# Self-attention of a perceiver: two batches at a time in tiles of 64 rows and columns, instead of one batch with two heads stacked

## The reference

```python
def _L0_attn_ref(x, qkv_w, proj_w, proj_b, slopes):      # head size 16
    q, k, v = (x @ qkv_w.T) split and by head             # rotary on q and k
    attn = einsum('bhqd,bhkd->bhqk', q, k) * 16 ** -0.5
    attn = attn + minimum(key - query, 0) * slopes[h] * 8.0
    out = einsum('bhqk,bhkd->bhqd', softmax(attn), v)
    return out @ proj_w.T + proj_b

def _L1_attn_ref(x, Wq, Wk, Wv, Wo):                      # head size 64
    scores = einsum('bhqd,bhkd->bhqk', Q, K) / 8          # rotary on Q and K
    scores = where(|query - key| <= 16, scores, -inf)
    return einsum('bhqk,bhkd->bhqd', softmax(scores), V) @ Wo
```

## Time and profile before

| what | value |
|---|---|
| time, median of 3 runs | 5175.37 us (5174.06 to 5181.66) |
| the profiled execution: its own time | 5172.16 us |
| its span | 5170.4 us |
| mean granted clock of PE | 0.928 |
| `attend_batches`, tag a0: PE's first product to the end of ACT's last copy | 829.4 to 943.6 us |
| `attend_batches`, tag a1: the same | 2702.9 to 2881.3 us |

### The profile page before, as it was taken

How to read it: one execution, slowest core, us unless ns; L and a number is a source line. 1 busy time by engine, 2 the same in 40 slices (tenths; PEclk the granted TensorE clock), 3 DMA queues, 4 the chain that set the end, 5 groups by cost and what they waited for, 6 DMA issues and landing times. The chain is left out here.

```text
span 5170.4 us, 144361 instructions
## 1 busy us (share of the span) xinstructions
PE 4547.7 (88%) x65130; PEld 3576.7 (69%) x65130; DVE 2497.3 (48%) x4406; ACT 1971.9 (38%) x3916; POOL 605.4 (12%) x392
## 2 busy tenths in 40 slices
PE   6999988699999799999799579999962669999968
PEld 5777776588888577888646447777742558888744
DVE  3555545566666455555434425555525145555531
ACT  3554541233333344444303114555431134444430
POOL 1111101000000011111031011111102021111000
PEclk9999996699999899999898799999975889999979
DMA  1111100121111111111000011111012511111000
GB/s 65 41 41 39 37 15 14 38 66 49 49 49 47 57 35 42 37 41 42 34 19 0 17 36 40 41 41 41 28 24 75 201 62 35 42 42 36 23 19 18
DMA packets 86893, 216.58 MB, mean 42 GB/s; under 512 B 28240, under 2 KB 51536, under 8 KB 83584
## 3 DMA queue, kind: packets, MB, share of 16 engines
q1 hardware_dynamic: 85536, 205.51, 12.3%
q0 software_dynamic: 768, 2.10, 0.1%
HBM read 198.26 MB, written 9.32 MB: 40 GB/s over the span
## 5 line engine op out<-in xcount | busy, mean ns | idle before, releaser
L679 DVE TENSOR_REDUCE x_pm<-banks 128x4 f32<-128x1536 f32 (+2 forms) x512 | 935.6, 1827 | 687.9 <-PE banks L582 687.9
L776 ACT ACTIVATE x_pl<-banks 128x384 f32<-128x384 f32 x1536 | 628.8, 498 | 705.3 <-PE banks L565 705.3
L506 POOL TENSOR_TENSOR x_cl<-xnT,x_ch 128x1601 fp32r<-128x1601 f32 x120 | 400.6, 3339 | 3291.2 <-ACT x_ch L791 3291.2
L781 ACT ACTIVATE x_kT<-banks,x_bk 128x384 f32<-128x384 f32 (+2 forms) x512 | 305.1, 596 | 560.6 <-PE banks L593 560.6
L603 PE MATMUL banks<-x_wh,x_ch 128*128 128x256 f32 (+1 forms) x1664 | 490.6, 295 | 0.0
L593 PE MATMUL banks<-x_ch,x_wh 128*128 128x384 f32 (+2 forms) x1024 | 410.7, 401 | 87.7 <-POOL x_v L513 86.6
L565 PE MATMUL banks<-x_q,x_kT 32*128 32x128 f32 x13312 | 482.3, 277 | 3.6 <-issue 3.6
L582 PE MATMUL banks<-x_kT,x_q 32*128 32x384 f32 (+2 forms) x4096 | 457.6, 511 | 13.8 <-DVE x_v L711 9.0
L603 PE MATMUL banks<-x_wh,x_cl 128*128 128x256 f32 (+1 forms) x1664 | 469.2, 282 | 0.0
L603 PE MATMUL banks<-x_wl,x_ch 128*128 128x256 f32 (+1 forms) x1664 | 467.7, 281 | 0.0
L565 PEld LDWEIGHTS banks<-x_q,x_kT 32*128 32x128 f32 x13312 | 436.2, 185 | 7.8 <-issue 5.2
(11 more groups left out here) (341 smaller groups left out, 7207.1 us busy)
## 6 DMA issues: line engine op xcount, KB each, us to landing
xnT<-in_ctxT SPq DMA_DIRECT2D x120, 800.5 KB, 4.3
e_w<-in_L_pack SPq DMA_DIRECT2D x91, 384.0 KB, 3.1
e_w<-in_L_pack SPq DMA_DIRECT2D x21, 1154.0 KB, 5.6
actT<-in_ctxT SPq DMA_DIRECT2D x8, 800.5 KB, 7.4
e_rw<-routed_rows SPq DMA_DIRECT2D x64, 64.0 KB, 2.8
x_rows<-e_zero SPq DMA_DIRECT2D x1, 2688.0 KB, 9.8
e_xt<-x_rows SPq DMA_DIRECT2D x21, 128.0 KB, 5.3
y_rows<-e_y SPq DMA_DIRECT2D x21, 128.0 KB, 1.7
```

The costliest lines, as they stand in the source:

```text
L506: nc.gpsimd.tensor_tensor(cl[:, u, k, 0:CTX], staged(b, k), ch[:, u, k, 0:CTX], ALU.subtract).then_inc(low_done, 1)
L679: nc.vector.tensor_reduce(pm[:, c, :, g], src[:, :, 0:hi - lo], AX.X, ALU.max).then_inc(max_done, 1)
L776: nc.scalar.activation(probabilities(c, j, lo, hi).rearrange("p t q -> p (t q)"), mine[j][:, 0:(hi - lo) * P], ACT.Exp).then_inc(exp_done, 1)
L781: nc.scalar.activation(kT[:, c, lo:hi], mine[1 if g == 0 and inside(b if c else b - 1) else 0][:, 0:hi - lo], ACT.Identity, bias=col[:, c: ...
```

## The change

`attend_batches` is replaced by `attend_pairs`, and the host's arrangement of four weight arrays changes with it.

- A step takes two batches. The 128 partitions of the scores are the 64 queries of one batch and the 64 of the other, and the free axis has all 16 heads: 128 x 1024.
- The scores are 32 products per pair of batches (L929), each one head of one batch: in a1 64 rows by 64 columns with 64 moving columns, in a0 32 rows by 64 columns. The scale goes into the DVE instruction that adds the bias (L995 in a0, L999 in a1). In a0 the masked copies of the queries are made once for all batches (`qm`, L1047); in a1 there are none, and the bias is read from `dist` by all heads. There is nothing left for POOL.
- The values of all 16 batches are made ahead of the first scores (L935), each batch in two halves of the heads, which lie on partitions 0 to 63 and 64 to 127; ACT copies them to `v` (L1050).
- The probabilities of a pair are transposed in 8 blocks (L945) and copied out of PSUM by ACT (L1056), not DVE. The product by the values is 32 products of 64 rows by 64 columns (L957), with 16 moving columns in a0 and 64 in a1.
- DVE scales the result in one instruction (L1019), and PE transposes it back (`turn_back`, L966: 2 blocks in a0, 8 in a1) in place of the product by `stack2`; ACT writes it out (L1042).
- The loop over the batches is written out. The value weights lie in `net.qT`, and come in two DMAs.

The core of the diff (the removed function is the one printed above):

```diff
-        attend_batches(net, tag, width, chunks, wts[4], extra_bias, qT, kT, ahead)
+        attend_pairs(net, tag, width, chunks, wts[4], extra_bias, qT, kT, ahead)
...
+    BLOCKS = HEADS // 2
+    F = BLOCKS * width
+    N = B // 2
...
+        x_ps = net.ps[2]
+        o_ps = net.ps[3].rearrange("p (o n) -> p o n", o=2)[:, :, 0:F]
...
+            qm = net.sb(tag + "_qm", [P, 2, chunks, TOK], ctx=mem)
+            s_ps = net.quads[0][:, :, 0:4 * S].rearrange("p j (h s) -> p j h s", s=S)
+        else:
+            s_ps = net.ps[0].rearrange("p (j h s) -> p j h s", j=2, s=S)
+
+        def place(h):
+
+            if extra_bias == "alibi":
+                return h % 8 // 2, h // 8 * 2 + h % 2
+            return h % 2, h // 2
...
+        @block.tensor
+        def _(pe):
+            def scores(n):
+                if n:
+                    pe.wait_ge(biased, n)
+                elif extra_bias == "alibi":
+                    pe.wait_ge(masked, 2)
+                for h in range(HEADS):
+                    j, at = place(h)
+                    for e in range(2):
+                        tok = slice((2 * n + e) * S, (2 * n + e + 1) * S)
+                        if extra_bias == "alibi":
+                            r = slice(32 * j, 32 * j + 32)
+                            left, right = qm[r, h % 2, h // 8, tok], kT[r, h // 8, tok]
+                        else:
+                            r = slice(64 * j, 64 * j + 64)
+                            left, right = qT[r, at, tok], kT[r, at, tok]
+                        last = nc.tensor.matmul(s_ps[e * S:(e + 1) * S, j, at], left, right, start=True, stop=True)
+                last.then_inc(s_full, 1)
+
+            def values(b):
+                for half in range(2):
+                    for k in range(KC):
+                        last = nc.tensor.matmul(net.bank(b % 8)[half * S:(half + 1) * S, 0:F], net.xnT[:, k, b * S:(b + 1) * S],
+                                                w[:, half, k], start=(k == 0), stop=(k == KC - 1))
+                last.then_inc(v_full, 1)
+
+            def turn(n):
+                pe.wait_ge(p_ready, n + 1)
+                if n >= 2:
+                    pe.wait_ge(done, n - 1)
+                flat = sc[:, n % 2].rearrange("p h s -> p (h s)")
+                for i in range(BLOCKS):
+                    last = nc.tensor.transpose(x_ps[:, i * P:(i + 1) * P], flat[:, i * P:(i + 1) * P], net.ident[:])
+                last.then_inc(turned, 1)
+
+            def attend(n):
+                pe.wait_ge(pt_ready, n + 1)
+                pe.wait_ge(v_ready, 2 * n + 2)
+                if n:
+                    pe.wait_ge(o_ready, n)
+                for i in range(BLOCKS):
+                    for e in range(2):
+                        for half in range(2):
+                            r = slice(half * S, (half + 1) * S)
+                            last = nc.tensor.matmul(o_ps[e * S:(e + 1) * S, half, i * width:(i + 1) * width],
+                                                    pT[r, i, e * S:(e + 1) * S], v[r, 2 * n + e, i * width:(i + 1) * width],
+                                                    start=True, stop=True)
+                last.then_inc(o_full, 1)
+
+            def turn_back(n):
+                pe.wait_ge(o_ready, n + 1)
+                flat = o[:].rearrange("p o i f -> p (o i f)")
+                for c in range(chunks):
+                    last = nc.tensor.transpose(x_ps[:, c * P:(c + 1) * P], flat[:, c * P:(c + 1) * P], net.ident[:])
+                last.then_inc(back_turned, 1)
+
+            pe.wait_ge(w_in, 32)
+            for b in range(B):
+                if b >= 8:
+                    pe.wait_ge(v_ready, b - 7)
+                values(b)
+            pe.wait_ge(v_ready, B)
+            scores(0)
+            for n in range(N):
+                turn(n)
+                if n + 1 < N:
+                    scores(n + 1)
+                if n:
+                    pe.wait_ge(pt_ready, n + 1)
+                    turn_back(n - 1)
+                attend(n)
+            pe.wait_ge(done, N - 1)
+            turn_back(N - 1)
+
+        @block.vector
+        def _(dve):
+            def shift_scores(n):
+                u = n % 2
+                dve.wait_ge(s_full, n + 1)
+                if n >= 2:
+                    dve.wait_ge(turned, n - 1)
+                if extra_bias == "alibi":
+                    nc.vector.scalar_tensor_tensor(sc[:, u].rearrange("p (j h) s -> p j (h s)", j=4), net.quads[0][:, :, 0:4 * S],
+                                                   0.25, bias[:].rearrange("p (j h) s -> p j (h s)", j=4), ALU.mult,
+                                                   ALU.add).then_inc(biased, 1)
+                else:
+                    nc.vector.scalar_tensor_tensor(sc[:, u], net.ps[0].rearrange("p (h s) -> p h s", s=S), 0.125,
+                                                   spread(dist[:].unsqueeze(1), (P, HEADS, S)), ALU.mult,
+                                                   ALU.add).then_inc(biased, 1)
+                dve.wait_ge(biased, n + 1)
+                nc.vector.tensor_reduce(mx[:], sc[:, u], AX.X, ALU.max).then_inc(maxed, 1)
+                dve.wait_ge(maxed, n + 1)
+                nc.vector.tensor_tensor(sc[:, u], sc[:, u], per_head(mx[:]), ALU.subtract).then_inc(soft, 1)
+
+            def add_up(n):
+                dve.wait_ge(p_ready, n + 1)
+                nc.vector.tensor_reduce(sums[:], sc[:, n % 2], AX.X, ALU.add).then_inc(added, 1)
+                dve.wait_ge(added, n + 1)
+                nc.vector.reciprocal(rs[:, n % 2], sums[:]).then_inc(inverted, 1)
+
+            def divide(n):
+                dve.wait_ge(o_full, n + 1)
+                dve.wait_ge(inverted, n + 1)
+                if n:
+                    dve.wait_ge(back_turned, n)
+                scale = rs[:, n % 2].rearrange("p (i o) -> p o i", o=2).unsqueeze(3)
+                nc.vector.tensor_tensor(o[:], o_ps.rearrange("p o (i f) -> p o i f", f=width),
+                                        spread(scale, (P, 2, BLOCKS, width)), ALU.mult).then_inc(o_ready, 1)
+
+            dve.wait_ge(tab_in, 32 if extra_bias == "alibi" else 16)
+            if extra_bias == "alibi":
+                nc.vector.tensor_tensor(bias[:], spread(dist[:].unsqueeze(1), (P, HEADS, S)), per_head(slopes[:]),
+                                        ALU.mult).then_inc(bias_ready, 1)
+                dve.wait_ge(bias_ready, 1)
+            shift_scores(0)
+            for n in range(N):
+                if n + 1 < N:
+                    shift_scores(n + 1)
+                add_up(n)
+                divide(n)
+
+        @block.scalar
+        def _(act):
+            def exps(n):
+                act.wait_ge(soft, n + 1)
+                nc.scalar.activation(sc[:, n % 2], sc[:, n % 2], ACT.Exp).then_inc(p_ready, 1)
+
+            def output(n):
+                act.wait_ge(back_turned, n + 1)
+                nc.scalar.activation(net.actT[:, 0:chunks, n * P:(n + 1) * P],
+                                     x_ps[:, 0:chunks * P].rearrange("p (c s) -> p c s", s=P), ACT.Copy).then_inc(done, 1)
+
+            if extra_bias == "alibi":
+                for e in range(2):
+                    nc.scalar.activation(qm[:, e], qT[:], ACT.Copy, scale=net.parity[:, 12 + e:13 + e]).then_inc(masked, 1)
+            for b in range(B):
+                act.wait_ge(v_full, b + 1)
+                nc.scalar.activation(v[:, b], net.bank(b % 8)[:, 0:F], ACT.Copy).then_inc(v_ready, 1)
+            exps(0)
+            for n in range(N):
+                act.wait_ge(turned, n + 1)
+                if n:
+                    act.wait_ge(o_full, n)
+                nc.scalar.activation(pT[:].rearrange("p i n -> p (i n)"), x_ps, ACT.Copy).then_inc(pt_ready, 1)
+                if n + 1 < N:
+                    exps(n + 1)
+                if n:
+                    output(n - 1)
+            output(N - 1)
...
-        self_attention(net, "a0", 32, 2, ...
+        self_attention(net, "a0", 16, 2, ...
...
-            self_attention(net, "a1", 128, 8, ...
+            self_attention(net, "a1", 64, 8, ...
```

214 lines of the change are left out of this document (36 added, 178 removed).

## The result

The changed kernel takes 5091.98 us (median of 4 runs, 5086.99 to 5098.59), the kernel before 5178.51 (median of 4 on the same chip, 5174.06 to 5183.73). The ratio is 0.983, with a 95% interval of 0.9811 to 0.9848: 1.7% faster. The forecast was 5085 with a range of 5062 to 5118.

The account below looks back on a forecast made before the run. PE's own work was taken to bound both stages; a0 23.1 us and a1 67.0 us less, together 90.1, took 5172.16 to 5082, and the median's 3.2 us above that execution gave 5085, range 5062 to 5118.

Parts of the forecast that it names:

- The bound: Stages a0 and a1 before the change: PE's own work sets both, busy 109.94 of 114.2 and 160.05 of 178.4 us.
- L612's price: Scores and product by the values: 0.0165 us a record at clock 1.00, 0.033 at 0.50, from four column groups in turn.
- Slower than before: tiles of 64*64 run one by one: Rival, chance 0.06: small tiles do not overlap, about 0.107 us a record at clock 0.50; total 5260 us.
- break-even of 0.08 us a record: Small records of both stages: the change turns from gain to loss at about this price at clock 0.50, over 2,048 records.
- The ring: Step period: transposes, scores, three DVE instructions, exponential, output; a1 10.0 us at clock 0.50, 8.1 at 1.00; a0 9.4, 7.5.
- The clock: Pairs' steps: a0 at 0.50 throughout, 9.4 us a step; a1 half at 0.50, half at 1.00, 9.1 us a step.
- Values of a1: L935 ahead of the pairs: 128 records with halves side by side, 27.5 us plus 3.5 for the cold clock, 31 us.
- from the last value to the first transposes: Before the first pair's transposes: first scores, DVE's three instructions, exponential, last value copy; 7.1 us in a1, 7.4 in a0.
- ends: Close of each stage, from the last pair's transposes to the last output: 10.2 us in a1, 7.6 in a0.
- The second DMA of the weights: Start of each stage: one more DMA issue, some 0.4 us in each.
- The sum: Both stages: a0 91.1 us against 114.2, a1 111.4 against 178.4, together 90.1 us less.
- rival of the higher clock: Rival, chance 0.10: a1 at 8.1 and a0 at 7.5 us a step, with shorter ends; total 5058 us.

Follow-up runs that it names:

- one tile in a row: Changed kernel with the loops of scores and product by the values turned, so neighbouring small products use the same rows and columns of the array; 5166.8 us, ratio 0.9979.
- scores two ahead: Changed kernel with scores(1) issued ahead of the loop and scores(n+2) after turn(n), a pair further ahead; 5041.15 us, ratio 0.973.
- values between the pairs: Changed kernel with only a1's first pair's values made ahead, the others behind each pair's product by the values; 5047.02 us, ratio 0.9743.
- both waits filled: Changed kernel plus four unread products of 256 columns behind each pair's product by the values, in both stages; 5064.42 us, ratio 0.9788.

## Why the prediction was right

**The bound.** That PE's own work bounds both stages before, and so halving it pays, was right. PE's busy time in the stages fell from 270 us to 135, and the run with one tile in a row shows it from the other side: with PE's work near its old size the gain is 0.2%. Once halved, PE's work is no longer the bound, as the prediction said.

**The price of the small records.** I took L612's price, 64 records 2.12 us at clock 0.50 and 1.06 at 1.00. Measured: 1.99 and 1.16 in a1, 1.57 at 0.50 for a0's scores and 1.91 for its product. So in a1 they were sized within 0.13 us either way and in a0 up to 0.55 us too dear. The choice of a row in which four groups took turns, made although no row had both groupings, was the step on which everything hung, and the experiments settled it: 5.99, 3.32 and 1.99 us for one, two and four tiles. That the groups would overlap in both directions was argued from rows; that one record would cost the same as in L612's tiles of another shape was not, and that it came so close was luck.

**"Slower than before: tiles of 64*64 run one by one"**, the rival on the other side, had 0.107 us a record at 0.50 and a total of 5260. (By its own words, half of 0.122 scaled by the clock, it would be 0.122.) Forced to happen for the scores and the product by the values, it was 0.090 us, PE's step in a1 15.6 us instead of 18.4, and 5166.8: still slightly faster than before, so the break-even of 0.08 us a record was too strict. But the rival also had the halves of L935 one after the other, 27 us more in a1 by the forecast, and that run left them in turn. Grouping them cost 16.6 us in the stages and still left some overlap; added up, which no run did, that would be some 5183 us against the 5176 of before. So its sign may have been right, and its size was too large.

**The ring.** Right in its members and their order, and in both of its ends at full clock: 8.14 us against 8.1, and 7.35 against 7.5. At 0.50 the forecast was 0.7 us too long in a0 (8.72 against 9.4, of which 0.55 are the scores), and some 0.2 us in a1 (9.8 in the longest steps, against 10.0).

**The clock.** Half and half for a1, 0.50 for a0: a1's steps had 0.76 between the first and the last `turn`, so half and half was right for the mean, but the period was 9.39, not 9.1. The mean of the clock is no weight for the period, because it matters which rows fall under which level. In the step shown above the clock is at 0.50 from 2741.2 to 2744.6 us, under the transposes and the scores, which are PE's part of the ring, and back at 1.00 for the product by the values, which isn't. a0 stayed at 0.50 from 860.5 us on, as forecast from its being at 0.50 before though busy; with the scores two ahead 14 us without any wait were at 0.50 as well, but a fill brought most of it to 1.00, and the forecast had no reason against that. The Trainium skill, page "TensorE: Matmul & The Clock Gate", section "Part 4: PE-mode transpose", would have a clock that transposes do not raise. No run here has steps of transposes alone; with the values between the pairs the clock stays at 1.00 through a1's 16 transposes a step, but with other products beside them. So it stays with the earlier trace rows, which speak against the rule.

**The other terms.** Values of a1 29.5 us against 31; of a0 8.9 against 10.3; from the last value to the first transposes 6.9 in a1 against 7.1 and 6.5 in a0 against 7.4; ends 11.0 and 7.3 against 10.2 and 7.6. The second DMA of the weights: PE waits 8.77 us for them in a1 where it waited 8.43, and 6.07 in a0 where it waited 6.21; I had 0.4 for each.

**The sum.** a0 came out 7.7 us shorter than forecast and a1 1.7 longer: the stages gave 6 us more than my 90. The 7 us by which the median is above 5085 are therefore not a term of the sum. They lie in the rest of the program, whose length one profile does not tell to better than the spread above, and in the kernel before, whose median of four is 3 us above the one that I started from. So the total is nearer than its parts: an error of 6 us one way was met by 13 us the other way, and that is luck. The rival of the higher clock, 5058, was near in its price: with both waits filled, and the clock at 0.86 and 0.92 in the steps, the kernel takes 5064.42, and the stages 182.0 us where that rival would have some 175.

## What to carry to other kernels

When a change halves an engine's work, write down the ring of the steps as well as the engines' sums: here no engine's sum was the period afterwards, and issuing one group of products a step earlier was worth another 42 us in the stages, where the change itself gave 96. Small products on parts of the array paid here only because neighbours in the program use different parts (1.7% against 0.2%); look at the order in which the loops emit them before changing anything else. And where an idle stretch on TensorE lets the clock fall, it costs more than itself: the values of a1 took 29.5 us ahead of the loop, and put into the waits they made the stage 36 us shorter.

## What the runs showed of the hardware

Four tiles of 64*64 in turn take a third of the time of the same records on one tile (1.99 against 5.99 us), two take 3.32, whether they differ in rows or in columns. Work that nothing reads, put into TensorE's waits, shortened a1 by 9.5 us through the granted clock (0.73 to 0.92 in its steps), small tiles as well as large; and yet small products on one tile at a time, busy for 97% of 122 us, left it at 0.50, and so did a0's small tiles in turn with transposes, busy for 14.00 of 14.00 us. What the clock looks at, so that all of this is true, is open: no run has steps of large products without waits, or a small fill in a0. Outside the two stages, with the same code, the time at 0.50 varied from 565 to 647 us between executions, and the program's length with it.
